# The large change of one call: order of the gelu split, the late graph work and step 4's attention

## What is computed

```
def _L0_gnn_ref(node_features, adjacency_matrix, attn_w, attn_b, W1, b1, W2, b2, g1, beta1, g2, beta2):
    mask = adjacency_matrix.astype(jnp.float32) + jnp.eye(n, dtype=jnp.float32) > 0
    for l in range(attn_w.shape[0]):
        si = x @ attn_w[l, :d]
        sj = x @ attn_w[l, d:]
        scores = si[:, :, None] + sj[:, None, :] + attn_b[l]
        scores = jnp.where(scores >= 0, scores, 0.2 * scores)
        scores = jnp.where(mask, scores, -jnp.inf)
        agg = jnp.einsum('bij,bjd->bid', jax.nn.softmax(scores, axis=-1), x)
        h = layernorm(x + agg, g1[l], beta1[l])
        ff = jax.nn.gelu(h @ W1[l] + b1[l], approximate=False) @ W2[l] + b2[l]
        x = layernorm(h + ff, g2[l], beta2[l])
...
def _L1_gnn_ref(h, W, a, adj):
    Wh = jnp.matmul(h, W)
    e = _leaky((Wh @ a1)[:, :, None] + (Wh @ a2)[:, None, :])
    attention = jax.nn.softmax(jnp.where(adj > 0, e, -9e15), axis=1)
    return _leaky(jnp.einsum('bij,bjf->bif', attention, Wh))
...
h = jnp.maximum(_layernorm(x, axis=-1), 0.0)
x = x + _L0_gnn_ref(h, adj, ...)
h = jnp.maximum(_layernorm(x, axis=-1), 0.0)
x = x + _L1_gnn_ref(h, L1_gnn_W, L1_gnn_a, adj)
```

## Time and profile before

| | us |
|---|---|
| three runs | 2034.87, 2035.45, 2035.59; median 2035.45 |
| the profiled execution | 2034.0, its span 2032.2 |
| PE busy | 1862.5 (92%) |
| DVE busy | 1560.6 (77%) |
| ACT busy | 1252.4 (62%) |
| POOL busy | 881.7 (43%) |

### The profile page before, as it was taken

How to read it: one execution, slowest core, us unless ns; L and a number is a source line. 1 busy time by engine, 2 the same in 40 slices (tenths; PEclk the granted TensorE clock), 3 DMA queues, 4 the chain that set the end, 5 groups by cost and what they waited for, 6 DMA issues and landing times.

```text
span 2032.2 us, 30833 instructions
## 1 busy us (share of the span) xinstructions
PE 1862.5 (92%) x11009; PEld 1586.9 (78%) x11009; DVE 1560.6 (77%) x4927; ACT 1252.4 (62%) x1948; POOL 881.7 (43%) x703
## 2 busy tenths in 40 slices
PE   3899999999899989999899998999989999999995
PEld 2787777888788878888778887788877888788884
DVE  6678887688777797778877689677887688777755
ACT  2566666666657565675665666756666666666562
POOL 3355453435433444343534354433453435433450
PEclk9899999999999999999999999999999999999998
...
DMA packets 40625, 52.33 MB, mean 26 GB/s; under 512 B 2926, under 2 KB 30872, under 8 KB 40472
## 3 DMA queue, kind: packets, MB, share of 16 engines
...
## 4 chain that ended last, share of the span: by engine, by line
PE 44%; DVE 36%; POOL 8%; ACT 7%; issue 5%; DMA 0%; DVEq 0%; ACTq 0%; POOLq 0%
PE acc L426 12%; PE acc L493 11%; PE ps_u L465 7%; PE acc L530 5%; POOL columns L1263 5%; DVE probs L938 4%; PE acc L512 3%; DVE junk L906 3%; DVE probs L1071 2%; DVE stats L998 2%; DVE probs L1075 2%; PE ps_t L389 2%; DVE stats L852 2%; DVE normed L970 2%; DVE h_lo L977 1%
## 5 line engine op out<-in xcount | busy, mean ns | idle before, releaser
L493 PE MATMUL acc<-w_hi,gelu_hi 128*128 128x256 f32 x1536 | 463.6, 302 | 17.3 <-POOL gelu_lo L1297 17.3
L723 ACT ACTIVATE g_full<-ps_u,vec_all 128x512 f32<-128x512 f32 x384 | 259.5, 689 | 330.7 <-PE ps_u L465 164.4
L1297 POOL TENSOR_TENSOR gelu_lo<-g_full,gelu_hi 128x512 fp32r<-128x512 f32 x240 | 310.1, 1301 | 313.1 <-ACT gelu_hi L731 253.5
L493 PE MATMUL acc<-w_hi,gelu_lo 128*128 128x256 f32 x1536 | 432.6, 282 | 0.0
L493 PE MATMUL acc<-w_lo,gelu_hi 128*128 128x256 f32 x1536 | 431.9, 281 | 0.0
L426 PE MATMUL acc<-x_nat,probs 128*128 128x257 f32 x1536 | 377.7, 394 | 54.3 <-DVE normed L951 27.1
L426 PEld LDWEIGHTS acc<-x_nat,probs 128*128 128x128 f32 x1536 | 279.5, 191 | 149.8 <-ACT probs L698 43.8
L1263 POOL TENSOR_TENSOR columns<-columns 128x4 f32<-128x4 f32 x128 | 135.8, 1061 | 563.9 <-DVE columns L867 563.9
L493 PEld LDWEIGHTS acc<-w_hi,gelu_hi 128*128 128x128 f32 x1536 | 290.9, 189 | 35.2 <-POOL gelu_lo L1297 29.4
L493 PEld LDWEIGHTS acc<-w_lo,gelu_hi 128*128 128x128 f32 x1536 | 291.7, 190 | 6.1
L493 PEld LDWEIGHTS acc<-w_hi,gelu_lo 128*128 128x128 f32 x1536 | 290.3, 189 | 0.0
...
## 6 DMA issues: line engine op xcount, KB each, us to landing
...
```

Source lines behind the costliest of these rows:

```text
L493: last = pe.matmul(acc[side][c // 2][:, cols:cols + D], h[:, r, tok], w[:, layer, f, :], start=False, stop=(f == FC - 1 and i == 2), skip_ ...
L723: full = act.activation(g_full[:, f % 2, :], ps_u[f % 2][:, :], ACT.Gelu, bias=b1_col[:, layer, f:f + 1])
L1297: pool.tensor_tensor(gelu_lo[:, f % RING, :], g_full[:, f % 2, :], gelu_hi[:, f % RING, :].bitcast(F32), ALU.subtract).then_inc(lo_done[0] ...
```

## The change

Every engine's order changes; nothing is computed in another way, and no instruction is added or taken away except for table loads that follow ACT's order.

- Steps 0, 1, 3 and 5: DVE's `gelu_high` stands in front of the variance, and POOL's `gelu_rest(0)` in front of the pow (there and in the closing step).
- Step 0: ACT makes low_row ahead of `final_apply`, and puts the copies of wh and the exps in turn.
- Steps 1 and 3: PE's down 2 and `scores_row` stand in front of all of `final_out`; DVE's two `final_scale` stand behind the scores; ACT does three of the four `final_exps` there and one at the end of the step before (2 and 2 until now). In steps 0 and 2, `h_rest` on DVE comes one round of `final_bounded`'s loop earlier.
- Step 2: on PE bound_rows stands behind down 2 and not in front; on ACT `final_h` in front of low_row.
- Step 4: on PE the attention follows up 6 directly, down 4 stands behind it, and the turn of the tokens in front of down 6.
- Step 5: DVE sums chunks 0 and 1 of the attention ahead of `input_stats`.
- Steps 4 and 5: the last mask chunk is made ahead of the attention norm's scaling (behind its variance), not behind it.

```diff
@@ PE, slot @@
                 if s.late is not None:
+                    down(n, side, layer, 2)
+                    scores_row(n + 1)
                     final_out(s.late[0], free, (0, 1), n - 1)
-                if s.late is not None:
-                    scores_row(n + 1)
                     final_out(s.late[0], free, (2, 3))
                 early_turn = s.final is not None and not soon
                 if early_turn:
                     final_turn(s.final[0], free, n)
-                if soon or early_turn:
+                if soon:
                     bound_rows(n + 1)
-                down(n, side, layer, 2)
+                if s.late is None:
+                    down(n, side, layer, 2)
+                if early_turn:
+                    bound_rows(n + 1)
...
                 up(n, layer, 6)
-                if s.prepare is not None and side == 0:
-                    down(n, side, layer, 4)
...
                 attend_out(n + 1, other, s.layer_a, graph_a)
-                if not (s.prepare is not None and side == 0):
-                    down(n, side, layer, 4)
+                down(n, side, layer, 4)
...
-                late_turn = (s.prepare is not None and side == 0)
+                late_turn = False
@@ ACT, pair_body @@
-                        final_exps(s.late[0], (2, 3))
+                        final_exps(s.late[0], (1, 2, 3))
...
                     if early_turn:
+                        final_h(s.final[0], free)
                         low_row(n + 1)
-                        final_h(s.final[0], free)
                     gelu(n, layer, 4)
                     if s.final is not None and s.layer_a == 0:
+                        low_row(n + 1)
                         final_apply(*s.final)
...
                     if s.final is not None and s.layer_a == 0:
                         final_h(s.final[0], free)
-                        final_wh(s.final[0], free)
-                    exps(n + 1)
+                        for c in range(NC):
+                            final_wh(s.final[0], free, (c,))
+                            exps(n + 1, (c,))
+                    else:
+                        exps(n + 1)
...
-                        final_exps(s.final[0], (0, 1))
+                        final_exps(s.final[0], (0,))
@@ DVE, attention_sum @@
+                if statistics is not None:
+                    sum_of(0)
+                    sum_of(1)
+                    input_stats(*statistics)
+                for c in range(NC):
+                    if statistics is None or c >= 2:
+                        sum_of(c)
...
@@ DVE, ff_norm @@
+                if follows and (scores is None or late is not None):
+                    gelu_high(n + 1)
                 variance(ln2_chain, n)
-                if follows:
+                if follows and scores is not None and late is None:
                     gelu_high(n + 1)
-                if late is not None:
-                    final_scale(late, 0)
...
-                if late is not None:
-                    final_scale(late, 1)
...
+                if late is not None:
+                    final_scale(late, 0)
+                    final_scale(late, 1)
@@ DVE, final_bounded @@
-                if step is not None:
-                    h_rest(*step)
+                    if step is not None and j == 1:
+                        h_rest(*step)
@@ DVE, pair_body @@
+                    if s.prepare is not None:
+                        prepare_masks(s.prepare, s.side, (3,))
                     attention_norm(n + 1)
                     if s.prepare is not None:
-                        prepare_masks(s.prepare, s.side, (3,))
                         layer_scores(n + 2, s.side, s.prepare, (n + 1, s.layer_a))
@@ POOL, pair_body @@
+                    low_first = s.begins or s.late is not None or not s.attend or s.layer_a == 0
+                    if low_first:
+                        gelu_rest(n, 0)
                     if not s.begins:
                         inverse_root(ln2_chain, n - 1, ln2_rstd)
-                    gelu_rest(n, 0)
+                    if not low_first:
+                        gelu_rest(n, 0)
```

22 lines of the change are left out of this document (12 added, 10 removed).

## The result

The changed kernel takes 2064.94 us (median of 4 runs, 2061.51 to 2067.64) against 2035.16 us before (4 runs): ratio 1.0149, 95% interval 1.013 to 1.0169. It is slower by about 30 us, outside the stated range (2016 to 2051), though on the forecast side of no change. The profiled execution has a span of 2063.2 us, 31.0 more than before.

A forecast was written before the change was run, and what follows sets the result against it. PE, busy 92% of the span, was taken to set the time. Seven pairs -2.5 us, closing step +0.3 and PE's clock +7.3 made +5.1 on 2035.45: 2040.5 us, range 2016 to 2051.

The forecast's parts named there:

- the chains: All steps without PE's clock level: -0.35 us a pair, seven times -2.5, and +0.3 in the closing step.
- the clock: Longer PE waits in steps 5 and 0 bring 7 more drops to 1.2 GHz, 1.04 us each: +7.3 us.
- Step 5: PE's attention ends sooner, but POOL's queue still sets the tokens' turn: -0.15 us (-1.0 to +0.3).
- Step 0: ACT's new order gains 0.6 us, a later turn costs 0.7: +0.1 us (-0.6 to +0.8).
- The hold on the variance: Steps 0, 1, 3, 5: gelu_lo 0 on POOL blocks DVE's two-input variance operations; pow starts 1.2 to 1.4 us later.
- Steps 1 and 3: Late gelu_lo 1 delays final_out by 1.05 us; 0.77 of slack leaves +0.25 us each; the g_full wait goes.
- Steps 2 and 4: Down 2 covers PE's wait for the maxima, -1.3 us; down 4 loses its cover behind the attention, +0.5.
- B: Whole kernel: as forecast, but PE's clock falls no oftener than now, 2033.3 us (2029 to 2036); chance 0.22.
- C: Steps 0, 1, 3, 5: variance gets through beside gelu_lo 0, 2001 us, or 2018 with half; chance 0.22.
- D: Steps 4 and 5: pow holds the masks operations moved beside it, 14 x 0.35 us, 2046 to 2051; chance 0.11.

The follow-up runs named there:

- e1: Changed kernel with needless matmuls put on PE where it waits in steps 5 and 0, nothing else moved: 2038.67 us, ratio 1.0027.
- e8: Changed kernel with the gelu order put back as before in all steps, every other edit kept: 2028.7 us, ratio 0.9977.
- e15: Kernel before with one edit, the new gelu order in steps 0, 1, 3 and 5: 2041.55 us, ratio 1.0036.
- e14: Kernel before with one edit, step 5's sums of chunks 0 and 1 ahead of input_stats: 2038.8 us, ratio 1.0022.
- e12: Changed kernel with DVE's input_stats back in front of the attention's sums in step 5: 2027.57 us (one run).
- e17: Kernel before with one edit, PE's down 2 and scores_row ahead of final_out in steps 1 and 3: 2045.32 us (one run).
- e5: Changed kernel with gelu_lo 2 waiting for DVE's shift and step 5's residual shift moved later, plus steps 1 and 3's gelu order undone: 2025.75 us, ratio 0.9955.
- e7: Kernel before with step 2's edit alone, on PE and ACT: 2022.89 us, ratio 0.995.
- e6: Changed kernel with gelu_lo 2 waiting for DVE's shift and step 5's residual shift moved later, plus PE's step 4 order undone: 2025.29 us, ratio 0.996.

## Why the prediction was wrong

The sum gave +5.1 us, of which the chains were -2.2 and the clock +7.3. Measured on the spans (+31.0), e1 puts the clock at 26.6 less the 2 x 1.04 that before had, about +24.5, and leaves about +6.5 for the chains. So some 17 of the 26 us missed are the clock, and the rest is in step 5 and in steps 1 and 3.

**The clock** was the term that failed most, in count and price. The mechanism was right (long waits of PE in steps 5 and 0, then a fall) and so were the places, but 7 more falls at 1.04 us were put down; there were 17 more, and a stretch costs 1.40 us (e1). The 3.62 us before the turn brought two stretches in a row in three pairs. And one wait in step 5 was overlooked, the 2.08 us before bound_rows, behind which three steps 5 fall early. The gelu order makes it: it is 0.32 us at most before and in e8, and 2.09 in e15. The prediction followed that order's hold into steps 0, 1 and 3 and put it at nothing in step 5. That a stretch costs more now, because PE no longer works between waits for y0 and y1 in it, is argued, not shown.

**Step 5** (-0.15 forecast): the chain over POOL was the right one, and it was followed as a queue only. Two terms are missing in it. The pow of the inputs was put at 1004.37 of the earlier trace rows, 26.13 us after the step's start, and came at 26.85, 0.7 later; in e8, without the gelu order, it comes at 26.20. So this is again that order's price at the step's start. The other 0.43 us is the hold: POOL's residual shift lies on the attention norm's own variance, the very fact on which the second paragraph of the prediction rests, and it was not applied here. Together they move the norm from 33.35, where the bare chain would have it, to 34.47, and PE waits 3.6 us, not 2.8. e14 and e12 show that without the sums ahead of input_stats there is no such wait, and that they alone make one of 3.38 us.

**Step 0** (+0.1): the hold and the wait were forecast as they came (1.83 us against 1.9 to 2.1). Without a fall the step is at its old length in e1 (41.88), as predicted, and the 0.6 us for ACT's new order are what e8 and e14 show. That pair 2 came out 1.1 us shorter turns on 0.24 us on ACT, which nothing in the prediction foresaw.

**The hold on the variance** came as forecast in length and place, but on another operation: the one that takes 1.15 us is L867, which has one input; the three in front of it, with two inputs each, had started before gelu_lo 0 did. The condition that the prediction read from its rows, two inputs in SBUF, was too narrow.

**Steps 1 and 3** (+0.25): the slack of 0.77 was the right yardstick, but what uses it up is PE's order ahead of final_out (e17), not the gelu order (e15, e5). The wait of 0.79 for g_full did not go either: it is 0.80 after.

**Steps 2 and 4** (-1.3, +0.5): right, with their reasons: step 2 alone gives 9 us (e7), and the attention of step 4 still waits for y0 and y1:

```profile
1225.93 2.01 PE L426 MATMUL acc<-x_nat,probs 128*128 128x257 f32 x8 [0.40 <-DVE normed L955]
1228.28 2.01 PE L426 MATMUL acc<-x_nat,probs 128*128 128x257 f32 x8 [0.34 <-DVE normed L955]
```

PE's order in step 4 costs 1.15 us (e6), where 1.42 less 0.15 was put down; no row gives the 0.15. What the prediction did not see is that this order gives 0.9 us back in step 5 (e6).

**The rivals.** B gave the change without the clock as -2; e1 shows +4 us. C is out: L867 of the variance was held, for 1.15 us or more, in every step with the gelu order. D is out: in all 14 places L881 and L883 keep 0.29 and 0.22 us beside the pow (in pair 4's step 5, 1272.40 to 1273.47), while L881 takes 1.25 to 1.27 us beside gelu_lo 7 in the seven steps 3. The Trainium skill's rule (SBUF — State Buffer, Who interferes with whom) would have them blocked, since both read two inputs in SBUF while POOL reads SBUF; for this pow on 128x4 values the measurement says otherwise.

**What the range missed**: undoing either the sums (e12) or the gelu order (e8) takes 35 to 37 us off, while alone they cost about 5 and 8 us (e14, e15). Their costs do not add: a late chain in step 5 is paid back in step 0, as the pow's start shows in e14 and e8, as long as that step has slack and the clock stays up.
